# A decoder layer whose start, last rows and expert loads are put in another order

## The reference

```
x = x + self_attention(layernorm(x))            # 16 heads of 32, causal; one weight for q, k, v; dense; biases
x = x + cross_attention(layernorm(x), ctx, ctx) # 16 heads of 32, padding mask, softmax; Wq, Wk, Wv, Wo; biases
x = x + experts(layernorm(x))

def experts(x):                                 # 8 experts, the best one per token
    probs = softmax(x @ Wg + bg); best = argmax(probs)
    h = gelu(x @ W1[best] + b1[best])
    return probs[best] * (h @ W2[best] + b2[best])
```

## Time and profile before

| | us |
|---|---|
| median of three runs | 2006.78 |
| the three runs | 2004.78, 2006.78, 2011.36 |
| the profiled execution, its own time | 2010.81 |
| its span, from the first to the last instruction | 2009.0 |
| busy in the span: TensorE / VectorE / ScalarE / GpSimd | 1878.4 / 1340.8 / 1129.2 / 977.3 |

### The profile page before, as it was taken

The page is one execution under the profiler, slowest core; times in us unless marked ns, Lnnn a source line. Parts: engine busy times, 40 slices in busy tenths (PEclk is TensorE's granted clock), DMA queues, the critical chain, the costliest instruction groups (busy, mean ns, idle before and its releaser), DMA issues. The chain is left out here.

```text
span 2009.0 us, 34915 instructions
## 1 busy us (share of the span) xinstructions
PE 1878.4 (93%) x10950; PEld 1324.0 (66%) x10950; DVE 1340.8 (67%) x2841; ACT 1129.2 (56%) x2164; POOL 977.3 (49%) x1148
## 2 busy tenths in 40 slices
PE   2899999999999999999999999999999854999997
PEld 1667777777777766666666666666666343898896
DVE  3567676666767676767575757576765336788886
ACT  3355554555555565556555656555655413787885
POOL 3255455455456455545444545555454423345454
PEclk9999999999999999999999999999999877999999
DMA  5434545546455564444454545445343369423220
GB/s 194 116 90 111 137 104 129 127 110 140 115 121 111 138 180 118 114 124 109 104 125 106 126 106 119 114 99 124 88 102 77 77 174 359 133 78 91 82 85 18
DMA packets 138090, 239.97 MB, mean 119 GB/s; under 512 B 31114, under 2 KB 32434, under 8 KB 137872
## 3 DMA queue, kind: packets, MB, share of 16 engines
q1 hardware_dynamic: 105728, 191.00, 35.0%
q0 software_dynamic: 21968, 46.42, 12.1%
q10 hardware_dynamic: 10240, 0.64, 0.4%
HBM read 115.63 MB, written 50.02 MB: 82 GB/s over the span
## 5 line engine op out<-in xcount | busy, mean ns | idle before, releaser
L535 ACT ACTIVATE attn_probs<-attn_sT 128x512 f32<-128x512 f32 (+3 forms) x1024 | 529.3, 519 | 470.7 <-PE attn_sT L826 467.3
L442 POOL TENSOR_TENSOR attn_probs<-attn_probs 128x512 f32<-128x512 f32 (+2 forms) x384 | 531.2, 1402 | 174.4 <-PE attn_o_ps L841 126.2
L641 DVE TENSOR_REDUCE attn_m_col<-attn_sS 128x1 f32<-128x512 f32 x512 | 342.5, 687 | 192.3 <-PE attn_sS L810 184.5
L826 PE MATMUL attn_sT<-attn_stack 98*128 98x512 f32 (+2 forms) x1024 | 387.3, 389 | 2.8 <-ACT attn_probs L535 2.8
L810 PE MATMUL attn_sS<-attn_stack 97*128 97x512 f32 (+2 forms) x1024 | 369.4, 371 | 12.6 <-DMA attn_stack<-attn_stage 3.8
L647 DVE CUSTOM_DVE_ANT_0 attn_sS<-attn_sS,attn_cT_low 128x128 f32<-128x128 f32 x496 | 240.9, 504 | 173.1 <-PE attn_sS L810 169.4
L826 PEld LDWEIGHTS attn_sT<-attn_stack 98*128 98x128 f32 x1024 | 188.1, 189 | 210.2 <-ACT attn_probs L535 133.6
L430 POOL TENSOR_SCALAR_AFFINE_SELECT attn_probs<-attn_probs 128x256 f32<-128x256 f32 x256 | 119.6, 468 | 360.8 <-ACT attn_probs L535 360.7
L841 PE MATMUL attn_o_ps<-attn_probs,attn_V 128*32 128x512 f32 (+3 forms) x2048 | 233.8, 528 | 6.1 <-ACT attn_probs L535 3.6
L810 PEld LDWEIGHTS attn_sS<-attn_stack 97*128 97x128 f32 x1024 | 193.3, 190 | 68.5 <-DVE attn_m_col L641 15.1
L790 PE MATMUL attn_pj<-attn_xT_high,attn_w_high 128*128 128x512 f32 x384 | 154.1, 401 | 3.9 <-DVE attn_w_low L607 3.9
(11 more groups left out here) (195 smaller groups left out, 3679.8 us busy)
## 6 DMA issues: line engine op xcount, KB each, us to landing
attn_stack<-attn_stage SPq DMA_DIRECT2D x672, 128.0 KB, 2.3
attn_rows<-in_x_dram SPq DMA_DIRECT2D x64, 256.0 KB, 4.1
attn_rows<-x_after_self SPq DMA_DIRECT2D x64, 256.0 KB, 4.5
moe_w<-in_L_ffn_W_dram SPq DMA_DIRECT2D x16, 1024.0 KB, 14.3
attn_stack<-attn_stage POOLq DMA_DIRECT2D x96, 128.0 KB, 3.3
x_after_self<-attn_rows SPq DMA_DIRECT2D x32, 256.0 KB, 2.6
x_after_self<-in_L_attn_b_dense_dram POOLq DMA_DIRECT2D x32, 256.0 KB, 5.0
attn_rows<-in_ctx_dram SPq DMA_DIRECT2D x32, 256.0 KB, 3.0
```

The costliest lines, as they stand in the source:

```text
L442: pool.tensor_tensor(total, total, tile_of(n, kb)[:, js, q0:S], ALU.add).then_inc(added, 1)
L535: act.activation(tile_of(n, kb)[:, j, q0:S], sT[:, i % 2, q0:S], ACT.Exp, scale=SCALE).then_inc(exp_done, 1)
L641: dve.tensor_reduce(to, sS[:, k % 2], AX_X, ALU.max).then_inc(s_free, 1)
L826: pe.matmul(sT[:, i % 2, q0:S], stack[0:ROW_MAX + 1, n % 2, 1, j, kb * P:(kb + 1) * P], stack[0:ROW_MAX + 1, n % 2, 0, j, q0:S], start=Tru ...
```

## The change

- The start. All four tiles are measured, scaled and normalised first. The biases are loaded by SP, behind the weights. Each weight part has a buffer of its own. Part 0 is split before the tiles are turned, parts 1 to 3 behind them, and the dense part's low part is made at step (-2, 12). The first unit waits for part k at its chunk k. The copies of the cross-attention weights are issued at step 7 of groups 1 to 4. Waits for the constants and the mask move to where they are needed.
- TensorE multiplies the identity by itself into `o_ps`, which nobody reads then: twelve times first, and four times at steps (-3, 14), (-3, 15) and (-2, 0).
- The last rows. The four row loads of the last batch are issued at steps 4 to 7 of group 63, the fourth into another buffer; the output bias is loaded as a row, and VectorE adds it to the rows. GpSimd doesn't accumulate for this batch.
- The experts. SP loads experts 0 and 1 behind the tokens, and experts 2 to 7 once the first tile is gathered and the tokens' places are known.

```diff
 measured, scaled, normalized:
-        return None if t is None or (b < 0 and t < 2) else (b + 1, t)
+        return None if t is None or b < 0 else (b + 1, t)
...
+    LAST, SPARE = NB_ALL - 1, RING - 2
+    TRI_AT, BIAS_AT = ("tri", B + 1, 0), ("bias", LAST + 1, 0)
...
-        seq = [key for key in seq if in_batch(key[1])]
+        seq = [key for key in seq if in_batch(key[1]) and key != ("r", LAST, NB - 1)]
+        if e == SPARE:
+            seq.append(("r", LAST, NB - 1))
+        if e == RING - 1:
+            seq.append(BIAS_AT)
...
+            if key[:2] == ("r", LAST):
+                at_group, q = NG - 1, 4 + t
...
+    load_at.setdefault((NG - 2, 4), []).append(BIAS_AT)
...
-        raw_buffers = [probs[:, i].rearrange("p j s -> p (j s)") for i in range(3)]
+        raw_flat = probs[:].rearrange("p i j s -> p (i j s)")
+        raw_buffers = [raw_flat[:, 3 * D * k:3 * D * (k + 1)] for k in range(KT)] + [V[:, 1:VRING].rearrange("p t d -> p (t d)")]
...
 SyncE, start:
             for i in range(len(weights)):
-                if i >= 3:
-                    sp.wait_ge(raw_done, i - 2)
                 src, raw, _, _ = weight_views(i)
-                sp.dma_start(raw_dst(raw, src), src).then_inc(raw_loaded[i % 3], 16)
-            for i in range(4):
-                sp.dma_start(scratch_w[i], cross_weights[i]).then_inc(swap_copied, 16)
+                sp.dma_start(raw_dst(raw, src), src).then_inc(raw_loaded[i], 16)
+            load_biases(nc, sp, bias, const_loaded)
...
-            sp.wait_ge(const_step, N_STEP)
-            sp.wait_ge(mask_stored, 16)
 SyncE, steps:
+                if q == 7 and 1 <= n <= 4:
+                    sp.dma_start(scratch_w[n - 1], cross_weights[n - 1]).then_inc(swap_copied, 16)
...
-                sp.wait_ge(biased[t], 16 * NB_ALL)
+                sp.wait_ge(biased[t], 16 * LAST)
 GpSimd:
-            layernorm_scale(0, 0)
-            pool.wait_ge(ln_ready, 4)
+            for half in range(2):
+                layernorm_scale(0, half)
+            pool.wait_ge(ln_ready, 8)
...
-                if u and u[0] == "wo":
+                if u and u[0] == "wo" and u[1] != LAST:
                     add_bias(u[1], u[2])
 ScalarE:
-            load_biases(nc, act, bias, const_loaded)
...
             high_of_weights(0)
-            for t in range(2):
+            for t in range(NB):
                 normalize(0, t)
-            for i in range(1, 3):
-                high_of_weights(i)
             for n, q in steps:
                 if (n, q) == (-2, 1):
-                    for i in range(3, len(weights)):
+                    for i in range(1, len(weights)):
                         high_of_weights(i)
                     act.wait_ge(const_loaded, 16 * N_CONST)
+                if (n, q) == (-1, 0):
                     act.wait_ge(const_step, N_STEP)
                     act.wait_ge(raw_done, len(weights))
 VectorE, add_rows:
+                if b == LAST:
+                    wait_row(dve, BIAS_AT)
+                    dve.tensor_tensor(to, to, row_block(BIAS_AT), ALU.add).then_inc(last_biased, 1)
+                    dve.wait_ge(last_biased, t + 1)
                 wait_unit(dve, u)
 VectorE, start:
-            for t in range(2):
+            for t in range(NB):
                 row_stats(0, t)
-            for i in range(3):
-                low_of_weights(i)
+            low_of_weights(0)
             for n, q in steps:
                 if (n, q) == (-2, 1):
-                    for i in range(3, len(weights)):
+                    for i in range(1, KT):
                         low_of_weights(i)
                     dve.wait_ge(const_loaded, 16 * N_CONST)
-                    dve.wait_ge(const_step, N_STEP)
+                if (n, q) == (-2, 12):
+                    low_of_weights(KT)
+                if (n, q) == (-1, 0):
                     dve.wait_ge(tri_loaded, 16)
 TensorE:
-                        pe.wait_ge(raw_done, len(weights) if what == "wo" else KT)
+                        pe.wait_ge(raw_done, len(weights) if what == "wo" else 1 if u == units[0] else KT)
+                elif u == units[0]:
+                    pe.wait_ge(raw_done, k + 1)
...
+            def keep_busy(count):
+                for _ in range(count):
+                    pe.matmul(o_ps[:, 0:P], ident[:], ident[:], start=True, stop=True)
+
             pe.wait_ge(const_step, 6)
+            keep_busy(12)
             for n, q in steps:
+                if (n, q) in ((-3, 14), (-3, 15), (-2, 0)):
+                    keep_busy(4)
+                if (n, q) == (-1, 0):
+                    pe.wait_ge(const_step, 8)
 expert_layer, SyncE:
+    SOON = 2
-            for e in range(E):
-                if e < LENT:
-                    sp.wait_ge(loaded[weight_sem[e]], 16)
-                if e != LENT:
-                    load_weights(e)
+            for e in range(SOON):
+                sp.wait_ge(loaded[weight_sem[e]], 16)
+                load_weights(e)
             sp.wait_ge(experts_ready, 1)
...
             sp.wait_ge(placed, 4)
-            sp.wait_ge(loaded[weight_sem[LENT]], 16)
-            load_weights(LENT)
+            for e in range(SOON, E):
+                if e < NB:
+                    sp.wait_ge(loaded[weight_sem[e]], 16)
+                load_weights(e)
```

More of the change, by code:

```diff
@@ L109, in scaled @@
         half = ({(0, 15): 0, (1, 11): 1} if crosses(b + 1) else {(0, 15): 0, (1, 0): 1}).get((g, q))
-        return None if half is None or (b < 0 and half == 0) else (b + 1, half)
+        return None if half is None or b < 0 else (b + 1, half)
     def normalized(n, q):
@@ L154, in attention_layers @@
     RING = len(shares[True])
-    TRI_AT = ("tri", B + 1, 0)
+    LAST, SPARE = NB_ALL - 1, RING - 2
+    TRI_AT, BIAS_AT = ("tri", B + 1, 0), ("bias", LAST + 1, 0)
     row_at, row_before = {}, {}
@@ L220, in attention_layers @@
         o_ps = ps("o_ps", [P, S])
-        raw_loaded = [sem(f"raw_loaded_{i}") for i in range(3)]
+        raw_loaded = [sem(f"raw_loaded_{i}") for i in range(KT + 1)]
         raw_high, raw_done = sem("raw_high"), sem("raw_done")
@@ L241, in attention_layers @@
         o_copied, o_divided, oT_high, oT_ready = sem("o_copied"), sem("o_divided"), sem("oT_high"), sem("oT_ready")
-        summed, biased = sem("summed"), [sem(f"biased_{t}") for t in range(NB)]
+        summed, biased, last_biased = sem("summed"), [sem(f"biased_{t}") for t in range(NB)], sem("last_biased")
         stage_f32, stack_f32 = stage[:].bitcast(F32), stack[:].bitcast(F32)
@@ L309, in weight_views @@
             src, to, of = weights[i]
-            raw = raw_buffers[i % 3]
+            raw = raw_buffers[i]
             return src, raw, [to(W[h]) for h in range(2)], of(raw)
@@ L348, in load_row @@
                     sp.dma_start(row_block(key)[:, 0:S // 2], scratch_tri).then_inc(loaded, 16)
+                elif what == "bias":
+                    sp.dma_start(row_block(key), b_out.partition_broadcast(P)).then_inc(loaded, 16)
                 elif what == "c":
@@ L390, in _ @@
                         load_row(key)
+                if q == 7 and 1 <= n <= 4:
+                    sp.dma_start(scratch_w[n - 1], cross_weights[n - 1]).then_inc(swap_copied, 16)
                 if (n, q) == (FIRST_CROSS - G, 0):
+                    sp.wait_ge(mask_stored, 16)
                     sp.wait_ge(swap_copied, 16 * 4)
@@ L465, in _ @@
             pool.sem_inc(const_step, 1)
-            pool.wait_ge(const_loaded, 16 * N_CONST)
             for n, q in steps:
@@ L483, in _ @@
         def _(act):
-            load_biases(nc, act, bias, const_loaded)
             act.preload_act_table_set("natural_log_exp_and_others")
             def high_of_weights(i):
-                act.wait_ge(raw_loaded[i % 3], 16 * (i // 3 + 1))
+                act.wait_ge(raw_loaded[i], 16)
                 _, _, (high, _), raw = weight_views(i)
```

## The result

The changed kernel took 1985.15 us in the median of four runs (1978.93 to 1985.33), the kernel before 2008.05 in four runs beside it (2004.78 to 2011.36): a ratio of 0.9884 (95% interval 0.9865 to 0.9904). Run once more later, it gave 1979.72 (1975.78 to 1983.77) against 2006.80, 0.9867 (0.9851 to 0.9883). It is faster, as forecast, but by 23 to 27 us (1.2 to 1.3%) where the forecast was 36.7, and above the forecast range, whose upper end was 1979. The profiled execution took 1985.33 us, with a span of 1983.4, 25.6 us less than that of before.

What follows compares the result with a forecast made beforehand. TensorE was taken to bound the head-group loop, so gains lay where it stands still: 18.0 + 8.9 + 9.8 = 36.7 us off the profiled 2010.81 gave 1974.1, less 4.0 for that run's offset, 1970 us; range 1962 to 1979.

Steps and rivals of the forecast that it cites:

- Part A, the start: Kernel start: reordered loads and normalising bring the first projection unit from 46.15 to 27.4; 18.0 us won, bounds 15.5 and 20.5.
- Rival 1: Start: identity products raise TensorE's clock before the first unit, winning 20.3 us there, total 1968; chance 0.14.
- rival 4: Start: biases come late on SP's queue, 3 to 6 us of the start's gain lost, total 1975; chance 0.06.
- Part B, the seam: Between attention and experts: no row-load wait or bias accumulation, next block at 1630.7 against 1639.63; 8.9 us won.
- 3.1 + 2.9: Seam's end: last row store lands in 3.1 us, next block starts 2.9 us later, as after the accumulation before.
- Part C up to the first gather: Experts' block: fewer early weights let stores land sooner, first gather at 1692.45, 10.0 us earlier; 9.8 us net.
- Part C behind the gather: Experts' tiles: 12 MB loaded after the first gather need 33 us, hidden; scatters and gathers of three tiles at risk.
- Under TensorE's work: Experts' tiles: each late expert arrives every 5.5 us against 12.25 us per tile, so its load is hidden.
- rival 2: Experts' first tiles: the 12 MB hold up scatters and gathers, two round trips lose 8 us, total 1978; chance 0.11.
- gathers beside 2 MB: Experts' block: gathers landed in 2.1 to 5.7 us, some beside 2 MB of weights, cited against late first tiles.
- 21.13 us under full load: Before the first gather: wait from 1680.38 for the last 16-byte stores beside the rows, while queues carried expert weights.
- What is won at the start stays, because nothing behind it runs by anything but TensorE: Head groups after the start: TensorE alone sets the pace, so the start's 18.0 us last to the end.

Runs made afterwards that it cites:

- e1: The changed kernel with expert weights loaded as before (experts 0 to 2 and 4 to 7 behind the tokens): 1987.51 us, ratio 0.9894.
- e11: The changed kernel with experts 2, 4, 5 and 6 loaded once the stores beside the rows landed, 3 and 7 after the first gather: 1980.96 us, ratio 0.9871.
- e5: The changed kernel with the last rows as before (row loads behind stores, output bias accumulated by GpSimd): 1993.47 us, ratio 0.9927.
- e7: The changed kernel with one row load of group 62 moved to step 11 of group 61, ahead of the next heads' transfers: 1980.83 us, ratio 0.9862.
- e3: The changed kernel with identity products also in group 63, five at its start and one in each further step: 1979.61 us, ratio 0.9853.
- e14: The changed kernel itself run once more, nothing edited: 1979.72 us, ratio 0.9867.
- e4: The changed kernel without any identity products at the start: 1979.88 us, ratio 0.9863.

## Why the prediction went wrong

- **Part A, the start: right, 1 us small.** First unit at 25.97 where 27.4 was worked out, second 3.6 us behind it, and 19.0 us still there at group 61 for 18.0, within the bounds of 15.5 and 20.5. The shortest landing of a part and the count of VectorE's subtractions (5.51 us for three) carried it. Rival 1 was half true: the identity raised the clock at about 14, but it did not last. The Trainium skill's rule ("TensorE: Matmul & The Clock Gate", Part 1), halved by default and released by sustained activity, agrees with the rise at about 14; the rival counted only the rise, and not the fall at 20.9. The biases (rival 4) delayed nothing: the first unit waited for TensorE.
- **Part B, the seam: the mechanism right, the size off.** 11.7 us for 8.9, above the bounds of 8 and 10. The mis-sized term is the end: store landing and start of the next block together took 3.25 us from the issue at 1612.90, where 3.1 + 2.9 was forecast. The store landed in 2.7, so the 2.9 us that followed the accumulation's landing before are some 0.5 here.
- **Part C up to the first gather: right.** 10.6 us won for 9.8, first gather 52.2 us behind the block's start for 52.8. e1 (10.6 to 20.0 us with the weights back beside them) and the landings of 2.9 to 4.8 us without them show that the weights made the stores slow.
- **Part C behind the gather: wrong, this step failed.** "Under TensorE's work" held for the weights themselves, and what was called at risk, scatters and gathers of the first tiles, happened: 8.5 us, rival 2, which the prediction priced at 8 and gave 0.11. That its price fits is partly luck: it stood for two round trips 4 us late each, and the trace shows one stall, 6.05 us of TensorE in front of tile 3, with the low clock behind it. It took gathers beside 2 MB as evidence against; the row that counted was its own 21.13 us under full load. e1 gives 8.3 of it back, e11 4.9. Against the 10.6 won in front of the gather, part C as a whole brought 2.1 us where 9.8 were forecast. The Trainium skill's rule ("DMA: Bandwidth & Descriptors", section Queues, rings and completion order) pointed there, and the scatters' 7.1 to 9.0 us agree with it.
- **"What is won at the start stays, because nothing behind it runs by anything but TensorE": wrong in the last groups, in the profiled execution.** In group 63 no further group's work fills TensorE's waits for exponentials, and there its clock decides: 23.2 us at 0.50, 16.5 at 1.00. The profile of before had the high one, that of after the low one. This term, 6.6 us, was missed, and no rival had it. By the mean clock it is more frequent in the changed kernels (25 of 43 runs against 6 of 38), though before has only one profile to place it. It came without the new row loads (e5) and without the stall in group 62 (e7); with more work in the group (e3) it did not come. The profile of e14 lacks this term: its span is 32.2 us below that of before, where 36.7 were forecast, and 8.3 are lost behind the gather all the same. What in the changed kernel makes it more frequent stays open; no run put the start back as it was.

The sum then, with 1.0, 2.8 and 0.8 for what A, B and C up to the gather brought more: 36.7 + 1.0 + 2.8 + 0.8 + 0.2 - 8.5 - 7.4 = 25.6, the difference of the two spans.

## What to carry to other kernels

Here a burst of bulk loads made the small DMAs beside it late, the 16-byte stores by 8 to 15 us, the first scatters by 4, the first tile's gathered rows by 3 (e11). So before moving such a burst, write down which small transfers lie in its new place, and put its end ahead of the first one that someone waits for: moving 12 MB of it behind the gather gained 10.6 us and gave back 8.5, and taking a third of it away from there gave nothing as long as it still met the scatters. A stretch at the end of a loop, where the next iteration's work no longer fills TensorE, is not bound by throughput; look at its granted clock in more than one execution before summing gains across it. Filler products kept the high clock in group 63, where TensorE's waits are short and the work goes on; at the start and in front of tile 0, ahead of a pause, they won nothing.

## Not expected of the hardware

- One product of two 128 x 128 float32 matrices leaves two records (x24 for twelve products in 4.42 us); at the high clock four took 1.06 us, 0.26 us each.
- The same program gave group 63 at clock 1.00 and at 0.50 in two executions, and not one of four kernels' 20 runs with one more product per step had the low mean clock.
- The four stores that put 16 bytes beside each of 4096 rows land in 3 to 5 us alone and 10.6 to 20.0 beside weight loads at 380 GB/s.
- The granted clock's column read 1.00 in the first 26 us of e4, where matmuls 0.43 us apart show the low clock: at the start of a trace the pace is what tells.
